# First attention: the 13 value products of a head in one run, with the turning of the queries beside it

## The reference, cut to what matters

```
scores = einsum('bhtd,bhsd->bhts', q, k) * D ** -0.5      # D = 8
scores = scores + attn_mask[None, None, :, :]             # (256, 1601)
probs  = softmax(scores, axis=-1)
out    = einsum('bhts,bhsd->bhtd', probs, v)
x      = x + tanh(g) * (out.transpose(0, 2, 1, 3).reshape(B, T, E) @ Wo.T + bo)
```

## Time and profile before

| | |
|---|---|
| runs (us) | 3655.91, 3664.70, 3665.01; median 3664.7 |
| profiled execution (us) | 3656.69, its span 3654.9 |
| mean granted TensorE clock | 0.944 |
| TensorE matmul / weight load busy | 3270.2 us (89%) / 2085.8 us (57%) |
| VectorE / ScalarE / GpSimd busy | 2651.5 us (73%) / 2037.9 us (56%) / 764.2 us (21%) |
| `attend0` in the span | from the first turning at 159.1 us to the last copy of heads at 1086.3 us |

### The profile page before, as it was taken

The page is one execution under the profiler, slowest core; times in us unless marked ns, Lnnn a source line. Parts: engine busy times, 40 slices in busy tenths (PEclk is TensorE's granted clock), DMA queues, the critical chain, the costliest instruction groups (busy, mean ns, idle before and its releaser), DMA issues. The chain is left out here.

```text
span 3654.9 us, 105647 instructions
## 1 busy us (share of the span) xinstructions
PE 3270.2 (89%) x38223; PEld 2085.8 (57%) x38223; DVE 2651.5 (73%) x8433; ACT 2037.9 (56%) x3688; POOL 764.2 (21%) x951
## 2 busy tenths in 40 slices
PE   4599999999992759989999999899999999997799
PEld 4344444444442546667666666676666666665354
DVE  4466666665655348889888988898899888887443
ACT  2266665665650216667667767676667666665111
POOL 1000000000000014343333423433334334333000
PEclk8699999999995879999999999999999999998899
DMA  4400000000000010000000000000000000001000
GB/s 127 121 16 13 14 15 13 13 13 13 13 2 23 0 43 23 12 20 15 12 20 13 12 22 14 20 13 12 22 13 12 22 13 21 13 12 47 0 0 11
DMA packets 76121, 76.47 MB, mean 21 GB/s; under 512 B 8872, under 2 KB 70905, under 8 KB 75178
## 3 DMA queue, kind: packets, MB, share of 16 engines
q1 hardware_dynamic: 75690, 70.72, 6.9%
HBM read 62.80 MB, written 7.90 MB: 19 GB/s over the span
## 5 line engine op out<-in xcount | busy, mean ns | idle before, releaser
L200 ACT CAST probsT_hi<-psT 128x512 f16<-128x512 f32 (+1 forms) x1024 | 512.0, 502 | 534.1 <-PE psT L138 526.3
L779 DVE CUSTOM_DVE_ANT_0 a_junk<-psT,a_mask 128x384 f16<-128x384 f32 (+1 forms) x1024 | 547.6, 573 | 327.3 <-PE psT L659 313.3
L1306 POOL TENSOR_TENSOR y_lo<-y,y_hi 128x512 f16<-128x512 f32 (+1 forms) x520 | 461.6, 920 | 1105.2 <-ACT y_hi L1504 1105.0
L207 DVE TENSOR_TENSOR probsT_lo<-psT,probsT_hi 128x512 f16<-128x512 f32 (+1 forms) x1024 | 597.6, 584 | 82.0 <-ACT probsT_hi L200 81.8
L163 DVE CUSTOM_DVE_ANT_0 probs<-psS,a_mask 128x512 f32<-128x512 f32 (+1 forms) x1032 | 557.3, 568 | 37.1 <-PE psS L123 21.4
L741 ACT ACTIVATE a_probs<-psS 128x1024 f32<-128x1024 f32 (+2 forms) x512 | 442.1, 863 | 236.4 <-PE psS L684 236.4
L138 PE MATMUL psT<-ident,probs 128*128 128x128 f32 (+1 forms) x3328 | 544.4, 279 | 14.2 <-issue 12.9
L138 PEld LDWEIGHTS psT<-ident,probs 128*128 128x128 f32 (+1 forms) x3328 | 383.8, 142 | 103.9 <-issue 19.7
L184 ACT ACTIVATE probs<-probs,negmax 128x1601 f32<-128x1601 f32 x257 | 419.6, 1633 | 4.4 <-DVE negmax L178 1.9
L150 PE MATMUL psO<-values,probsT_hi 128*128 128x64 f16 (+1 forms) x3328 | 345.8, 193 | 11.4 <-DVE out L220 7.1
L123 PE MATMUL psS<-y_hi,q_hi 128*128 128x512 f16 (+1 forms) x1032 | 345.0, 334 | 1.9 <-DVE max L163 0.6
(11 more groups left out here) (259 smaller groups left out, 6266.9 us busy)
## 6 DMA issues: line engine op xcount, KB each, us to landing
head_w<-in_head_w SPq DMA_DIRECT2D x132, 161.0 KB, 2.2
a_kaug<-a_keys SPq DMA_DIRECT2D x288, 24.0 KB
ctx<-in_ctx SPq DMA_DIRECT2D x9, 768.0 KB
a_keys<-p_kst SPq DMA_DIRECT2D x8, 832.0 KB, 4.6
p_ctx<-in_ctx SPq DMA_DIRECT2D x8, 768.0 KB
a_kaug<-a_keys SPq DMA_DIRECT2D x96, 32.0 KB
p_mask_raw<-in_mask_t SPq DMA_DIRECT2D x6, 448.0 KB, 6.1
a_mask<-in_attn_mask SPq DMA_DIRECT2D x1, 2048.0 KB, 8.5
```

Source lines behind the costliest of these rows:

```text
L200: nc.scalar.copy(hi, src).then_inc(a.copied_hi, 1)
L207: nc.vector.tensor_tensor(lo, src, hi, ALU.subtract).then_inc(a.copied_lo, 1)
L779: nc.vector.tensor_tensor_reduce(junk[:, i % 2, 0:PIECE[j]], psA[i % 2][:, 0:PIECE[j]], mask[:, t, j, 0:PIECE[j]], 1.0, LOWEST, ALU.add, A ...
L1306: nc.gpsimd.tensor_tensor(w.y_lo[:, j, o:o + width], w.y32[:, o:o + width], w.y_hi[:, j, o:o + width], ALU.subtract).then_inc(keys_ready, 1)
```

## The change

`weigh` takes no slot any more: it waits for all four exponentials of its head and issues the 13 products in the order in which the chunks lie in `probs`, over the four column groups in turn. It is called once an iteration, in slot 1 after the forward matmuls. The turning of the queries moves from slot 0 to slot 1, behind it. On ScalarE the copy of the turned queries moves from slot 0 to slot 1, and the taking of the head's output from slot 3 to slot 2. The number of instructions of each kind stays as it is.

```diff
-VALUE_ORDER = [[0, 1, 4, 5], [2, 3, 6, 7], [8, 9, 12], [10, 11]]
-VALUE_COLS = [[0, 1, 2, 3], [0, 1, 2, 3], [0, 1, 2], [3, 0]]
...
-                def weigh(n, sl):
+                def weigh(n):
                     b, h = n // H, n % H
-                    if sl == 0 and n > 0:
+                    if n > 0:
                         pe.wait_ge(out_taken, n)
-                    pe.wait_ge(exp_done, 4 * n + sl + 1)
-                    for c, col in zip(VALUE_ORDER[sl], VALUE_COLS[sl]):
-                        at = SLOT_START[sl] + SLOT_ORDER[sl].index(c)
+                    pe.wait_ge(exp_done, 4 * n + 4)
+                    order = [c for slot in SLOT_ORDER for c in slot]
+                    for at, c in enumerate(order):
+                        col = at % 4
                         ins = nc.tensor.matmul(psO[32 * col:32 * col + VW, 0:T], w.values[:, b, c, h, :],
-                                               probs[:, n % 2, at, :], start=(sl == 0), stop=False,
+                                               probs[:, n % 2, at, :], start=(at < 4), stop=False,
                                                skip_group_check=True)
-                    if sl == 3:
-                        ins.then_inc(pv_done, 1)
+                    ins.then_inc(pv_done, 1)
...
-                        if 0 <= it - 1 < HEADS:
-                            weigh(it - 1, sl)
-                        if sl == 0 and turns(it):
+                        if sl == 1 and 0 <= it - 1 < HEADS:
+                            weigh(it - 1)
+                        if sl == 1 and turns(it):
                             turn_queries(it)
...
-                        if sl == 0 and turns(it):
+                        if sl == 1 and turns(it):
                             take_queries(it)
                         if sl == 2 and it >= 5 and it % 4 == 1:
                             take_heads(it)
-                        if sl == 3 and 0 <= it - 1 < HEADS:
+                        if sl == 2 and 0 <= it - 1 < HEADS:
                             take_out(it - 1)
```

## The result

| | before | after |
|---|---|---|
| median of the runs (us) | 3664.9 (4 runs, 3655.9 to 3666.8) | 3779.1 (4 runs, 3749.9 to 3785.5) |
| ratio, 95% interval | | 1.031 (1.026 to 1.036) |
| profiled execution, span (us) | 3654.9 | 3748.1 |
| mean granted clock of the span | 0.944 | 0.938 |

The kernel became slower by 3.1%, 114 us by the medians. The profiled execution is the quickest of the changed kernel; the other runs were granted a mean clock of 0.926 to 0.929 where it had 0.938.

A forecast was written before the change was run, and what follows sets the result against it. Forward matmuls would wait for VectorE's maxima to free two banks: 94 x 0.67 + 31 x 0.31, less two heads' gain, 72 us, plus 4 for clock, on 3656.7 gives 3733; 3737 us between profiled and median; range 3695 to 3785.

The forecast's parts named there:

- The layout of a head: One ordinary head timed from its value block's start: next block at 7.14 us against 6.47, +0.67.
- f6: First forward matmul of slot 3: held until VectorE's maximum frees its bank, start 3.80 us instead of 3.37.
- f7: Second forward matmul of slot 3: waits for a maximum to free its bank, start 4.28 us.
- f0: First forward matmul of slot 0, which opens at 4.54 us: start 5.22 us.
- f2: First forward matmul of slot 1: waits for a maximum, start 6.40 us, its own time being 6.30.
- f3: Second forward matmul of slot 1: waits for a maximum, start 6.88 us, before the next value block.
- f1: Second forward matmul of slot 0: waits for a maximum from slot 3, start 5.36 us.
- the clock: Term for lower granted clock around gatherings in the first attention: 4 us added, bounds 0 and 25.
- gatherings keep their number: Step behind the clock term: as many gatherings, with less value work close behind them, so only 4 us added.
- a stage clock below 0.95: Sign named beforehand: a mean clock of the first attention below 0.95 would make the prediction wrong.
- The faster case: Rival: maxima stay hidden and only draining counts, 0.35 us saved a head, 44 us in all, 3613 to 3621; chance 0.06.
- The clock rival: Rival: stretch without value work at half clock in most heads, about 2 us more each, up to 250 us; chance 0.05.

The follow-up runs named there:

- with short maxima the kernel before: Kernel before the change, each row maximum taken over the first 64 columns only (wrong maximum for the queries): 3660.4 us, ratio 1.000.
- the changed kernel with short maxima: Changed kernel, each row maximum taken over the first 64 columns only (wrong maximum for the queries): 3612.5 us, ratio 0.988 to the kernel before.

## Why the prediction was right, and where it was off

**The value block.** Predicted 2.05 from one round and the last head's run; it is 2.05.

**The layout of a head.** Predicted f6 3.80, f7 4.28, slot 0 4.54, f0 5.22, slot 1 5.62, f2 6.40, f3 6.88, next block 7.14 after the block's start. Measured 3.80, 4.28, 4.54, 5.23, 5.61, 6.41, 6.89, 7.15. The lags of the earlier trace rows carried over unchanged, in an order that the trace of before did not show. The one small miss: after a matmul that waited alone, the maximum follows 0.38 after the weight load (649.14 to 649.52) and not 0.46, which f1 profits from. On gathering heads this made 8.29 of the 8.38 predicted.

**The cause** is shown by taking it away in both kernels (0.988, with 1.23 us a head less) and by the pair without gathering, 86 us apart at full clock. The waits for maxima came to 131 us by the view of waits, predicted near 140.

**The term that was mis-sized is the clock.** I allowed 4 us for it with a bound of 25. On the profiled execution it was about 21, which puts that one at 93 instead of 76. On the other runs, with a clock lower by 0.01, it seems to have been some 30 more, which makes the median 114; no trace shows where these runs lost it. The step that failed is that "gatherings keep their number", and so nearly keep their cost: of the 30 in the stretch, 20 are followed by half clock instead of 11, 119 us of it instead of 58. A gathering now has no value products near it on either side, but that this is the reason is not shown, and one run speaks against it: with short maxima the kernel before keeps its value products where they were, and its stage clock is lower still, 0.91. The prediction had named a stage clock below 0.95 as a sign against it, and the clock came out at 0.94: the sign was right about this term and not about the waits. The bound of 25 held for the profiled execution only; the measured median, 42 us above the forecast of 3737, stayed inside the range because the upper end also had 25 us of lags in it that were not needed. The waits were forecast; that the time fell into the range as well was in part luck. A smaller slip: the closing chances (0.07 faster, 0.06 within, 0.87 slower) do not add up from those of the cases, which give 0.06, 0.05 and 0.89.

**The rivals.** The faster case fell: the drains are real, 0.27 a head once the maxima are short, but the maxima do not stay hidden. What the Trainium skill (TensorEngine Tiling (Array Packing), Key Properties) says of changing the tiling mode agrees with the 0.27 saved on three blocks fewer. So does its warning (the same page, PSUM Bottleneck) that tiling does not speed up the emptying of PSUM, with maxima that still follow one another by 0.48 to 0.55; here the second one decides. The clock rival in its strong form, a half clock in most heads, did not come; without gatherings there is none. The copy of the queries moved on ScalarE costs nothing: with the turning and this copy alone moved the time is the same. The moved taking of the output was not run alone; the changed kernel with short maxima has it, and its heads come out at 5.92 even so.

**What stays open.** Why more of the gatherings are followed by half clock after the change. Why the profiled execution of the changed kernel had a higher clock than its other runs. Runs of one kernel differ in it, and the traces show only one execution of each. Nor did I find what part of the split gathering's 39 us in the changed kernel is the split's own.

## What to carry to other kernels

When a producer on TensorE works through two PSUM banks that another engine reads, the filler work between its matmuls is not overhead: it is the reader's time. Before collecting such filler in one block to save drains, lay out one period with three lags from the trace (load to read, read to read, read to next load) and see whether the chain of two reads still fits between the pairs; the layout here was right to 0.01 us in 7. Then look at the clock of each variant beside its time: in the kernel before, a wait that was removed showed up in full in the time only after the thinnest piece of TensorE's work had been split and spread.

## What the runs showed of the hardware that I had not expected

A gathering is 16 matmuls of 9 columns in 1.9 us, whose weight loads follow one another without a break, and it can be enough to bring the clock down from 2.4 to 1.2 GHz shortly after. In the changed kernel the gathering at 662.65 is followed by this (the same columns; 663 to 666 us was still at 1.00):

```profile
666.00:670.00 4.00, 3.96 (x36) 1.59 (x36) 2.62 (x11) 2.05 (x2) 0.00 (x0) 0.58 0.02 4
```

How often it happens changes with how the gathering lies. Without gatherings the stage clock is 1.00 in both kernels; with them whole it is 0.91 to 0.96; in halves one slot apart, 1.3 and 1.6 us from the end of one to the start of the other, 0.99 and 0.98; in halves two slots apart, 3.2 us (704.92 to 708.15), 1.00, at the same amount of gathering. In the changed kernel, where the halves have no value products between them and lie 0.7 us apart, it is 0.95. That is not all there is to it: in the kernel before all gatherings have the same work around them, and 11 of 30 are followed by half clock. The Trainium skill (TensorE: Matmul & The Clock Gate, HAM oscillation) puts the fall of the clock down to idle gaps of TensorE; here it fell with no such gap, after thin work (TensorE is shown busy for all of the 3 us from 663 to 666).

And a faster order can lose its gain to the clock: with short maxima the kernel before saved 0.28 us on each head without a gathering and ended at the same time, its stage clock down from 0.96 to 0.91.
